# Gate logits of a mixture-of-experts layer from 12 float32 products per image in place of 36 bf16 products

## The chip, the cores and the metric

The kernel runs on one core of a Trainium2 chip. The metric is the device time of one execution in microseconds (us), lower is better.

## The reference

The input x is float32, 32 images of 384 channels and 28 x 28 = 784 pixels. The output is x plus a mixture of experts of its group normalisation:

```python
def _gn(v, G=32, eps=1e-5):
    B_, C_, H_, W_ = v.shape
    g = v.reshape(B_, G, C_ // G, H_, W_)
    m = jnp.mean(g, axis=(2, 3, 4), keepdims=True)
    s = jnp.var(g, axis=(2, 3, 4), keepdims=True)
    return ((g - m) / jnp.sqrt(s + eps)).reshape(v.shape)

x_flat = x.transpose(0, 2, 3, 1).reshape(-1, c)
scores = jax.nn.softmax(x_flat @ gate_w + gate_b, -1)      # 4 experts
top_v, top_i = jax.lax.top_k(scores, 2)
top_w = jax.nn.softmax(top_v, -1)
present = (top_i[:, :, None] == jnp.arange(e)[None, None, :]).any(0)
coef = jnp.einsum('ke,kbhw->ebhw', present.astype(x.dtype), wmap)
hdn = jax.nn.relu(jnp.einsum('bchw,edc->ebdhw', x, w1) + b1)
y = jnp.einsum('ebdhw,eod->ebohw', hdn, w2) + b2
out = jnp.einsum('ebohw,ebhw->bohw', y, coef)
```

`present` says of each rank (first or second choice) and expert whether any pixel at all chose it; the coefficient of an expert is the sum of the weights of the ranks in which it is present. The gate logits decide which expert is first and second, so they are computed with float32 accuracy.

## The kernel before

**Tiles.** Channels lie on the 128 partitions, three to a partition (NJ = 3). The images are taken in 8 groups of 4 (IMAGES). The 3136 pixels of a group are cut into 7 tiles of T = 448 pixels, and a tile times an expert is a unit: 28 units in a group, 224 in all. A unit has three chunks (NK) of the hidden dimension. For unit u TensorE computes `mm1(u + 1)`, that is 27 products of 448 columns into `z_ps`, and then `mm2(u)`, 27 products into `y_ps` (lines 444 to 486). Each float32 operand is held as two float32r numbers, `hi` and `lo` = value - `hi`, and each product is made of three: hi x lo, lo x hi, hi x hi. Between the two, VectorE scales a chunk by the coefficient row into `hid` (`scale`, line 508), ScalarE makes `h_hi` (line 515) and VectorE `h_lo` (line 519).

**Preparation of an image.** While one image is computed the next is prepared: VectorE takes statistics (`stats`, `group_stats`), GpSimd raises the variance to the power -0.5 (line 289), VectorE normalises the image in place in `x_raw`, half by half (line 303). ScalarE rounds it to `x_hi` (line 331), VectorE makes `x_lo` (line 335). For the gate the normalised half is split further into three bf16 parts, `x_part`: ScalarE casts part 1 (`part1`, line 308), VectorE subtracts it (`less_part1`, line 314), ScalarE casts part 2 (`part2`, line 319), VectorE subtracts that into part 3 (`part3`, line 323). The gate weights are split in the same way once (lines 605 to 608), and the three parts of the 4 experts stand in 12 of 32 stationary columns, `gw_part`.

**The gate product** (lines 338 to 348) is TensorE's: 3 parts x 3 channel slices x 4 quarters of the image. A quarter has 196 pixels, and its product is put at its own column tile of 32, so that its result stands in partitions 32 g to 32 g + 31 of one bank. ScalarE copies the result (`gate_copy`), VectorE transposes it, adds up the three parts (line 363) and the bias, and finds the two best (`gate_logits`, `gate_top2`, `gate_weights`, `gate_coefs`). The coefficient rows `wrow` go to HBM (`rows_out`) and come back broadcast over partitions (`rows_in`).

**What sets the order.** Every engine has its instructions in an order written out by hand, with semaphores between them. On VectorE and ScalarE the steps of the next image stand behind given chunks: `preparing` (line 567) turns the chunk number q into an offset `off` = q - (21 k - 30) for image k of the group, and `group` places, for example, `less_part1` of the first half at `off` 5, `part3` at 7 and 9, `gate_logits` at 12, and the second `split_x_lo` at `HI1[k]` + 1. TensorE has the gate product of image k ahead of `mm1` of unit 7 (k - 1) + 1, and that of image 1 ahead of unit 3. SyncE issues all loads and stores. `next_image` (line 909) waits until `x_lo` of the image that holds the place in `x_raw` is made. The numbers `SCAN_LINKS`, `IMAGE_LINKS` and `DVE_LINKS` count VectorE's chained steps for its own semaphore.

**The start.** Image 0 is prepared alone, while the weights arrive and are split (`weight_hi` on ScalarE, line 761, `weight_lo` on GpSimd, line 847). TensorE first runs WARM = 8 float32 products of 128 columns on a tile of ones (line 975). VectorE counts which experts were picked in image 0; if one is missing for a rank, a scan over the other images follows (not taken with this input). Image 1 is prepared in the first chunks of group 0 (`prepare_first`).

Of the kernel before, what the change touches and what calls it, by code (L numbers as in the profile page):

```python
# [21 lines left out]
PARTS = 3  # L22
# [8 lines left out]
WARM = 8  # L31
SCAN_LINKS = 38
IMAGE_LINKS = 32
# [21 lines left out]
def conv_moe(nc, x, gate_w, gate_b, w1, b1, w2, b2, out):  # L55
    f32, f32r, bf16, i32 = mybir.dt.float32, mybir.dt.float32r, mybir.dt.bfloat16, mybir.dt.int32
# [6 lines left out]
    with ctx:  # L63
# [14 lines left out]
        gw_part = sb("gw_part", [P, NJ, 32], bf16)  # L78
        gw_rest = sb("gw_rest", [P, 2, NJ, E])
# [7 lines left out]
        x_part = sb("x_part", [P, PARTS, HALVES, NJ, HALF], bf16)  # L87
        xn_rest = sb("xn_rest", [P, NJ, HALF])
# [8 lines left out]
        def slab_of(tile, i):  # L97
# [9 lines left out]
        early_rest = rows[:, 1, 1:1 + EARLY].rearrange("p r t -> p (r t)")[:, 0:NJ * HALF].rearrange(  # L107
            "p (j t) -> p j t", j=NJ)
# [83 lines left out]
        class Sems:  # L192

            def __init__(self, pre):
# [4 lines left out]
                self.part1_ready = sem(pre + "part1_ready")  # L199
                self.rest_ready = sem(pre + "rest_ready")  # L200
                self.part2_ready = sem(pre + "part2_ready")
                self.part3_ready = sem(pre + "part3_ready")
# [95 lines left out]
        def rest_of(h, alone):  # L298
            return early_rest if alone and h == 1 else xn_rest[:, :, :]

# [4 lines left out]

        def part1(act, s, n, q, h):
            act.wait_ge(s.xn_ready, HALVES * n + h + 1)
            nc.scalar.copy(x_part[:, 0, h], x_raw[:, q, :, half(h)]).then_inc(s.part1_ready, 1)  # L308

        def less_part1(dve, s, n, q, h, alone=False):  # L310
            dve.wait_ge(s.part1_ready, HALVES * n + h + 1)
            if h == 1 and not alone:
                dve.wait_ge(s.part3_ready, HALVES * n + 1)
            nc.vector.tensor_tensor(rest_of(h, alone), x_raw[:, q, :, half(h)], x_part[:, 0, h],  # L314
                                    ALU.subtract).then_inc(s.rest_ready, 1)

        def part2(act, s, n, h, alone=False):
            act.wait_ge(s.rest_ready, HALVES * n + h + 1)
            nc.scalar.copy(x_part[:, 1, h], rest_of(h, alone)).then_inc(s.part2_ready, 1)  # L319

        def part3(dve, s, n, h, alone=False):
            dve.wait_ge(s.part2_ready, HALVES * n + h + 1)
            nc.vector.tensor_tensor(x_part[:, 2, h], rest_of(h, alone), x_part[:, 1, h],  # L323
                                    ALU.subtract).then_inc(s.part3_ready, 1)
# [256 lines left out]
        def _(dve):  # L581
# [4 lines left out]
            nc.vector.memset(gw_part[:, :, :], 0.0)  # L586
# [12 lines left out]
            for i in range(NJ * HALVES):  # L599
# [30 lines left out]
            with dve.If(flag > 0):  # L630
                nc.vector.memset(pad[:, :], 0.0).then_inc(scan_free, 1)
                with dve.Fori(1, B) as b:
# [6 lines left out]
                    for h in range(HALVES):  # L639
                        normalise(dve, scan, n, 1, h)  # L640
                        less_part1(dve, scan, n, 1, h)
                        part3(dve, scan, n, h)
# [28 lines left out]
            def prepare_first(G, q, lk):  # L671
# [8 lines left out]
                if q == 2:  # L680
                    normalise(dve, main, 1, 1, 1)
                    less_part1(dve, main, 1, 1, 0)
                if q == 3:
                    split_x_lo(dve, 1, 1, 0)
                    part3(dve, main, 1, 0)
                    less_part1(dve, main, 1, 1, 1)
                if q == 4:
                    split_x_lo(dve, 1, 1, 1)
                    part3(dve, main, 1, 1)
# [9 lines left out]
            def group(G):  # L699
                lk = Links(dve, dve_step, G.g * DVE_LINKS + START[0] + (0 if G.first else EARLY_LINKS))  # L700
                for q in range(CHUNKS):
# [10 lines left out]
                    for k, off in preparing(G, q):  # L712
# [12 lines left out]
                        if off == 5:  # L725
                            less_part1(dve, main, n, slot, 0)
                        if off == 7:
                            part3(dve, main, n, 0)
                            less_part1(dve, main, n, slot, 1)
                        if off == 9:  # L730
                            part3(dve, main, n, 1)
# [25 lines left out]
        def _(act):  # L757
# [7 lines left out]
            for h in range(HALVES):  # L765
                part1(act, main, 0, 0, h)
            for h in range(HALVES):
                part2(act, main, 0, h, True)
            for h in range(HALVES):
# [15 lines left out]
            with act.If(flag > 0):  # L785
                with act.Fori(1, B) as b:
                    n = b - 1
                    for h in range(HALVES):
                        part1(act, scan, n, 1, h)
                        part2(act, scan, n, h)  # L790
# [3 lines left out]
            def prepare_first(G, q):  # L794
                if q == 2:
                    part1(act, main, 1, 1, 0)
                    split_x_hi(act, 1, 1, 0)
                if q == 3:
                    part2(act, main, 1, 0)
                    part1(act, main, 1, 1, 1)  # L800
                    split_x_hi(act, 1, 1, 1)
                if q == 4:
                    part2(act, main, 1, 1)
# [7 lines left out]
            def group(G):  # L811
                for q in range(CHUNKS):
# [3 lines left out]
                    for k, off in preparing(G, q):  # L816
                        n, slot = G.image(k), k % SLOTS
                        if off == 4:
                            part1(act, main, n, slot, 0)
                        if off == 5:  # L820
                            part1(act, main, n, slot, 1)
                        if off == 6:
                            part2(act, main, n, 0)
                        if off == 8:
                            part2(act, main, n, 1)
# [205 lines left out]
```

## Time and profile before

| | |
|---|---|
| median of 3 executions | 2565.67 us |
| lowest and highest | 2565.27 and 2566.45 us |
| profiled execution, its own time | 2567.38 us |
| its span, first to last instruction | 2565.6 us |
| mean granted clock of TensorE | 0.996 of full speed |
| TensorE busy | 2519.3 us, 98% of the span |
| VectorE busy | 1623.8 us, 63% |
| ScalarE busy | 630.7 us, 25% |
| DMA queue of loads and stores | 187.81 MB, 25.7% of 16 engines |

The span lies 1.8 us under that execution's own time. Busy shares are averages over stages with different limits: the first 110 us and the rest have to be read apart. Engines are named PE (TensorE), PEld (its weight loads), DVE (VectorE), ACT (ScalarE), POOL (GpSimd) and SP (SyncE); L344 is line 344 of the kernel before. An entry `A <- B` in a list of waits says that A's engine sat idle until B was done. Matmuls are pipelined: a duration of 0.36 us overlaps the next, and the distance between starts is what a product costs.

### The profile page before, as it was taken

To read this page: it belongs to the slowest core of one execution; us is meant where nothing else is said; L and a number is where in the kernel's file an instruction comes from. 1 tells how busy PE (TensorE), PEld (TensorE's weight loads), DVE (VectorE), ACT (ScalarE), POOL (GpSimd) and SP (SyncE) were. 2 spreads that over 40 slices of the span, in tenths; PEclk is the share of its full clock that TensorE was granted. 3 is DMA by queue.
4 is the path that set the end of the run, shared out by engine and by line. 5 is a ranking of instruction groups with operands and counts; after the bars stand their busy time and mean duration, and the time that the engine had idled before them with its cause. 6 is when DMAs were issued, how large, how long until landed. Compare 5 with 4: busy or idle time off the path is not lost.

```text
span 2565.6 us, 34840 instructions
## 1 busy us (share of the span) xinstructions
PE 2519.3 (98%) x13266; PEld 2302.0 (90%) x13266; DVE 1623.8 (63%) x3293; ACT 630.7 (25%) x973; POOL 74.4 (3%) x44
## 2 busy tenths in 40 slices
PE   4899999999999999999999999999999999999999
PEld 3799999999999999999999999999999999999998
DVE  7766666666666657665666666576666666665643
ACT  3322222222222222222222222222222222222211
POOL 3000000000000000000000000000000000000000
PEclk9999999999999999999999999999999999999999
DMA  4322123222133221232311322203322123231120
GB/s 161 89 78 71 52 70 89 78 82 59 52 89 93 67 79 55 69 100 68 92 55 46 100 78 82 80 25 97 89 71 78 51 72 100 61 91 51 46 75 22
DMA packets 193439, 190.15 MB, mean 74 GB/s; under 512 B 29808, under 2 KB 191856, under 8 KB 193264
## 3 DMA queue, kind: packets, MB, share of 16 engines
q1 hardware_dynamic: 193264, 187.81, 25.7%
q8 instruction: 111, 1.82, 0.3%
q14 instruction: 64, 0.52, 0.1%
HBM read 146.03 MB, written 41.75 MB: 73 GB/s over the span
## 4 chain that ended last, share of the span: by engine, by line
PE 96%; DVE 2%; DMA 1%; issue 1%; POOL 0%; ACT 0%; SPq 0%; DVEq 0%; POOLq 0%; ACTq 0%
PE y_ps L479 16%; PE y_ps L481 16%; PE z_ps L460 16%; PE y_ps L480 16%; PE z_ps L462 16%; PE z_ps L461 16%; PE g_ps L344 1%; DMA b_sb<-in_b 0%; DMA rows<-rows_dram 0%; DVE h_lo L519 0%; DVE x_part L323 0%; DVE x_lo L335 0%; POOL w_lo L847 0%; DVE x_raw L303 0%; DMA rows_dram<-wrow 0%
## 5 line engine op out<-in xcount | busy, mean ns | idle before, releaser
L508 DVE SCALAR_TENSOR_TENSOR hid<-z_ps,b_sb,rows 128x448 f32<-128x448 f32 x668 | 453.5, 679 | 753.9 <-PE z_ps L462 739.7
L479 PE MATMUL y_ps<-h_lo,w_hi 128*128 128x448 f32 x2016 | 741.8, 368 | 13.4 <-DVE h_lo L519 13.1
L460 PE MATMUL z_ps<-x_lo,w_hi 128*128 128x448 f32 x2016 | 743.4, 369 | 1.3 <-DVE x_lo L335 1.0
L481 PE MATMUL y_ps<-h_hi,w_hi 128*128 128x448 f32 x2016 | 741.1, 368 | 0.0
L480 PE MATMUL y_ps<-h_hi,w_lo 128*128 128x448 f32 x2016 | 740.9, 368 | 0.0
L462 PE MATMUL z_ps<-x_hi,w_hi 128*128 128x448 f32 x2016 | 736.7, 365 | 0.0
L461 PE MATMUL z_ps<-x_hi,w_lo 128*128 128x448 f32 x2016 | 736.5, 365 | 0.0
L515 ACT ACTIVATE h_hi<-hid 128x448 fp32r<-128x448 f32 x672 | 385.2, 578 | 1356.8 <-DVE hid L508 1343.2
L519 DVE SCALAR_TENSOR_TENSOR h_lo<-hid,h_hi 128x448 fp32r<-128x448 f32 x672 | 413.6, 616 | 26.5 <-ACT h_hi L515 26.1
L479 PEld LDWEIGHTS y_ps<-h_lo,w_hi 128*128 128x128 f32 x2016 | 379.3, 188 | 50.4 <-DVE h_lo L519 14.4
L460 PEld LDWEIGHTS z_ps<-x_lo,w_hi 128*128 128x128 f32 x2016 | 379.9, 188 | 38.0 <-issue 7.1
L481 PEld LDWEIGHTS y_ps<-h_hi,w_hi 128*128 128x128 f32 x2016 | 379.4, 188 | 35.5
L480 PEld LDWEIGHTS y_ps<-h_hi,w_lo 128*128 128x128 f32 x2016 | 379.3, 188 | 34.8
L462 PEld LDWEIGHTS z_ps<-x_hi,w_hi 128*128 128x128 f32 x2016 | 379.6, 188 | 33.1
L461 PEld LDWEIGHTS z_ps<-x_hi,w_lo 128*128 128x128 f32 x2016 | 380.2, 189 | 29.3
L534 DVE SCALAR_TENSOR_TENSOR res<-y_ps,bias,res 128x448 f32<-128x448 f32 x165 | 102.7, 677 | 101.7 <-PE y_ps L481 101.6
L289 POOL TENSOR_TENSOR rstd<-gvar_eps,minus_half 128x8 f32<-128x8 f32 x32 | 52.7, 1646 | 2286.3 <-DVE gvar_eps L284 2286.3
L319 ACT CAST x_part<-xn_rest 128x1176 bf16<-128x1176 f32 x63 | 73.9, 1173 | 135.7 <-DVE xn_rest L314 135.7
L526 DVE SCALAR_TENSOR_TENSOR res<-rows,bias_gap,res 128x448 f32<-128x448 f32 x168 | 104.7, 677 | 0.0
L308 ACT CAST x_part<-x_raw 128x1176 bf16<-128x1176 f32 x64 | 75.0, 1173 | 82.3 <-DVE x_raw L303 82.3
L267 DVE BATCH_NORM_STATS2 st<-x_raw 128x6 f32<-128x392 f32 x186 | 92.8, 554 | 2.3 <-DMA x_raw<-in_x 2.3
L314 DVE TENSOR_TENSOR xn_rest<-x_raw,x_part 128x1176 f32<-128x1176 f32 x63 | 86.9, 1380 | 3.5 <-ACT x_part L308 0.2
(97 smaller groups left out, 695.6 us busy)
## 6 DMA issues: line engine op xcount, KB each, us to landing
rows<-rows_dram SPq DMA_DIRECT2D x78, 560.0 KB, 7.4
x_raw<-in_x SPq DMA_DIRECT2D x62, 588.0 KB, 7.4
res<-in_x SPq DMA_DIRECT2D x80, 336.0 KB, 3.5
out<-res SPq DMA_DIRECT2D x78, 336.0 KB, 3.1
rows<-rows_dram SPq DMA_DIRECT2D x16, 840.0 KB, 7.2
res<-in_x SPq DMA_DIRECT2D x16, 504.0 KB, 5.8
out<-res SPq DMA_DIRECT2D x16, 504.0 KB, 6.0
rows<-rows_dram SPq DMA_DIRECT2D x16, 280.0 KB, 6.6
```

What stands on the lines that cost most here:

```text
L267: ins = nc.vector.bn_stats(st6[:, HALVES * j + h], x_raw[:, q, j, half(h)])
L460: nc.tensor.matmul(z, w1_hi[:, e, j, ks], lo, start=(j == 0), stop=False)
L461: nc.tensor.matmul(z, w1_lo[:, e, j, ks], hi, start=False, stop=False)
L462: ins = nc.tensor.matmul(z, w1_hi[:, e, j, ks], hi, start=False, stop=(j == NJ - 1))
L479: nc.tensor.matmul(y, w2_hi[:, e, k, ms], h_lo[:, slot], start=first, stop=False)
L480: nc.tensor.matmul(y, w2_lo[:, e, k, ms], h_hi[:, slot], start=False, stop=False)
L481: ins = nc.tensor.matmul(y, w2_hi[:, e, k, ms], h_hi[:, slot], start=False, stop=last)
L508: nc.vector.scalar_tensor_tensor(hid[:, q % HIDS], z_ps[:, q % ZB, 0:T], b1_sb[:, e, k:k + 1], coef, ALU.add, ALU.mult).then_inc(scaled, 1)
L515: nc.scalar.activation(h_hi[:, q % RING], hid[:, q % HIDS], ACT.Relu).then_inc(hhi_ready, 1)
L519: nc.vector.scalar_tensor_tensor(h_lo[:, q % RING], hid[:, q % HIDS], 0.0, h_hi[:, q % RING].bitcast(f32), ALU.max, ALU.subtract).then_inc ...
L526: lk.inc(nc.vector.scalar_tensor_tensor(xs, rows[:, G.slot(t), E], bias_gap[:, m:m + 1], xs, ALU.mult, ALU.add))
L534: nc.vector.scalar_tensor_tensor(xs, y_ps[:, m, 0:T], bias01[:, 1, m:m + 1], xs, ALU.add, ALU.add).then_inc(out_ready, 1)
```

## The change

The gate product multiplies the normalised pixels themselves, as they stand in `x_raw` in float32, with float32 gate weights padded to 32 columns (`gw_pad`): 3 channel slices x 4 quarters = 12 instructions, at the same column tiles. The three-part split of pixels and weights goes, with its four steps per half image (`part1`, `less_part1`, `part2`, `part3`), its buffers and semaphores, and the sum over the three parts in `gate_logits`. TensorE's gate product waits for `xn_ready` in place of `part3_ready`; since it now reads `x_raw`, SyncE waits for `gate_ready` too before it loads another image into the place. The warm-up has 12 products in place of 8 and waits for `rstd_ready` in place of `part1_ready`. The core of the diff (the calls of the four steps, which also go in the scan, in `prepare_first` and in `group` of both engines, are left out):

```diff
--- before.py
+++ after.py
@@
-WARM = 8
-SCAN_LINKS = 38
-IMAGE_LINKS = 32
+WARM = 12
+SCAN_LINKS = 37
+IMAGE_LINKS = 31
@@
-        gw_part = sb("gw_part", [P, NJ, 32], bf16)
-        gw_rest = sb("gw_rest", [P, 2, NJ, E])
+        gw_pad = sb("gw_pad", [P, NJ, 32])
@@
-        x_part = sb("x_part", [P, PARTS, HALVES, NJ, HALF], bf16)
-        xn_rest = sb("xn_rest", [P, NJ, HALF])
@@
-        def gate_product(pe, s, n):
-            pe.wait_ge(s.part3_ready, HALVES * (n + 1))
-            for t in reversed(range(PARTS)):
-                for j in range(NJ):
-                    for g in range(4):
-                        h, at = divmod(g * QUART, HALF)
-                        ins = nc.tensor.matmul(g_ps[32 * g:32 * (g + 1), 0:QUART], gw_part[:, j],
-                                               x_part[:, t, h, j, at:at + QUART],
-                                               start=(t == PARTS - 1 and j == 0), stop=(t == 0 and j == NJ - 1),
-                                               tile_position=(0, 32 * g))
+        def gate_product(pe, s, n, q):
+            pe.wait_ge(s.xn_ready, HALVES * (n + 1))
+            for j in range(NJ):
+                for g in range(4):
+                    ins = nc.tensor.matmul(g_ps[32 * g:32 * (g + 1), 0:QUART], gw_pad[:, j],
+                                           x_raw[:, q, j, g * QUART:(g + 1) * QUART],
+                                           start=(j == 0), stop=(j == NJ - 1), tile_position=(0, 32 * g))
             ins.then_inc(s.gate_ready, 1)
@@
-            lk.link(nc.vector.tensor_reduce(
-                lg[:, :, :], lg_pix[:, :, 0:PARTS * E].rearrange("p c (t e) -> p c e t", e=E), AX.X, ALU.add))
-            lk.link(nc.vector.tensor_tensor(lg[:, :, :], lg[:, :, :], over_pixels(gb[:, :]), ALU.add))
+            lk.link(nc.vector.tensor_tensor(lg[:, :, :], lg_pix[:, :, 0:E], over_pixels(gb[:, :]), ALU.add))
@@
-            lk.link(nc.vector.tensor_copy(gw_part[:, :, 0:E], gw_in[:, :, :]))
-            lk.link(nc.vector.tensor_tensor(gw_rest[:, 0], gw_in[:, :, :], gw_part[:, :, 0:E], ALU.subtract))
-            lk.link(nc.vector.tensor_copy(gw_part[:, :, E:2 * E], gw_rest[:, 0]))
-            nc.vector.tensor_tensor(gw_part[:, :, 2 * E:3 * E], gw_rest[:, 0], gw_part[:, :, E:2 * E],
-                                    ALU.subtract).then_inc(gw_ready, 1)
+            nc.vector.tensor_copy(gw_pad[:, :, 0:E], gw_in[:, :, :]).then_inc(gw_ready, 1)
@@
             for h in range(HALVES):
                 normalise(dve, main, 0, 0, h)
-            for h in range(HALVES):
-                less_part1(dve, main, 0, 0, h, True)
-            for h in range(HALVES):
-                part3(dve, main, 0, h, True)
@@
-            def next_image(b, place_free, k):
+            def next_image(b, place_free, gate_done, k):
                 sp.wait_ge(main.xlo_ready, place_free)
+                sp.wait_ge(main.gate_ready, gate_done)
@@
             pe.wait_ge(gw_ready, 1)
-            pe.wait_ge(main.part1_ready, 1)
+            pe.wait_ge(main.rstd_ready, 1)
             for _ in range(WARM):
                 nc.tensor.matmul(g_ps[:, 0:P], ones[:, :], ones[:, :], start=True, stop=True)
```

TensorE's instructions at the start, `ones` being the warm-up tile; the same replacement of the row of gate products stands at each of the 32 gate products. Before:

```order
L970 UNCONDITIONAL_BRANCH
L975 MATMUL g_ps<-ones 128x128 x8
L344 MATMUL g_ps<-x_part,gw_part 32x196 x36
L460 MATMUL z_ps<-x_lo,w_hi 128x448
L461 MATMUL z_ps<-x_hi,w_lo 128x448
L462 MATMUL z_ps<-x_hi,w_hi 128x448
```

and after the change:

```order
L895 UNCONDITIONAL_BRANCH
L900 MATMUL g_ps<-ones 128x128 x12
L309 MATMUL g_ps<-x_raw,gw_pad 32x196 x12
L422 MATMUL z_ps<-x_lo,w_hi 128x448
L423 MATMUL z_ps<-x_hi,w_lo 128x448
L424 MATMUL z_ps<-x_hi,w_hi 128x448
```

The row of 36 became one of 12 whose moving operand is `x_raw`; nothing moved against the z products.

VectorE's instructions during the preparation of image 1, from the second half's normalisation on. Before:

```order
L303 TENSOR_SCALAR x_raw<-x_raw,norm 128x3x392
L314 TENSOR_TENSOR xn_rest<-x_raw,x_part 128x1176
L508 SCALAR_TENSOR_TENSOR hid<-z_ps,b_sb,rows 128x448
L519 SCALAR_TENSOR_TENSOR h_lo<-hid,h_hi 128x448
L335 TENSOR_TENSOR x_lo<-x_raw,x_hi 128x3x392
L323 TENSOR_TENSOR x_part<-xn_rest,x_part 128x1176
L314 TENSOR_TENSOR xn_rest<-x_raw,x_part 128x1176
L508 SCALAR_TENSOR_TENSOR hid<-z_ps,b_sb,rows 128x448
L519 SCALAR_TENSOR_TENSOR h_lo<-hid,h_hi 128x448
L526 SCALAR_TENSOR_TENSOR res<-rows,bias_gap,res 128x448 x3
L335 TENSOR_TENSOR x_lo<-x_raw,x_hi 128x3x392
L323 TENSOR_TENSOR x_part<-xn_rest,x_part 128x1176
```

and after the change:

```order
L290 TENSOR_SCALAR x_raw<-x_raw,norm 128x3x392
L470 SCALAR_TENSOR_TENSOR hid<-z_ps,b_sb,rows 128x448
L481 SCALAR_TENSOR_TENSOR h_lo<-hid,h_hi 128x448
L302 TENSOR_TENSOR x_lo<-x_raw,x_hi 128x3x392
L470 SCALAR_TENSOR_TENSOR hid<-z_ps,b_sb,rows 128x448
L481 SCALAR_TENSOR_TENSOR h_lo<-hid,h_hi 128x448
L488 SCALAR_TENSOR_TENSOR res<-rows,bias_gap,res 128x448 x3
L302 TENSOR_TENSOR x_lo<-x_raw,x_hi 128x3x392
L470 SCALAR_TENSOR_TENSOR hid<-z_ps,b_sb,rows 128x448
```

The two L314 and the two L323 are gone; the rest keeps its order.

## Rows read from the trace of the kernel before

**Rows 1.** The page: busy us of each engine, and TensorE's granted clock in 40 slices

```profile
PE 2519.3 (98%) x13266; PEld 2302.0 (90%) x13266; DVE 1623.8 (63%) x3293; ACT 630.7 (25%) x973; POOL 74.4 (3%) x44
...
PEclk9999999999999999999999999999999999999999
```

**Rows 2.** Waits of TensorE, whole run: us in total, times, longest us

```profile
PE g_ps L975 <- ACT x_part L308: 22.2, 1, 22.2
PE y_ps L479 <- DVE h_lo L519: 13.1, 5, 6.4
```

**Rows 3.** The same, from 115 us to 2565 us

```profile
PE y_ps L479 <- DVE res L534: 0.3, 1, 0.3
PE g_ps L344 <- issue: 0.3, 1, 0.3
```

**Rows 4.** Timeline of TensorE, last gate product: start us, us, what, count

```profile
2411.70 0.36 PE L481 MATMUL y_ps<-h_hi,w_hi 128*128 128x448 f32 x1
2411.99 0.94 PE L344 MATMUL g_ps<-x_part,gw_part 128*32 128x196 bf16 x36
2412.86 0.48 PE L460 MATMUL z_ps<-x_lo,w_hi 128*128 128x448 f32 x1
2413.18 0.37 PE L461 MATMUL z_ps<-x_hi,w_lo 128*128 128x448 f32 x1
```

**Rows 5.** Instructions of the tile g_ps: count, duration ns min/median/max

```profile
L344 PE MATMUL g_ps<-x_part,gw_part x1152: 247/248/373, 27.5 to 2412.7; 128*32 128x196 bf16 x192
L352 ACT COPY lg_rows<-g_ps x32: 322/322/323, 29.2 to 2413.0; 128x196 f32<-128x196 f32 x32
...
L975 PE MATMUL g_ps<-ones x16: 421/421/552, 22.2 to 25.6; 128*128 128x128 f32 x16
```

**Rows 6.** Timeline of TensorE in the start, clock at 1.2 GHz: warm-up and first gate product

```profile
22.79 2.13 PE L975 MATMUL g_ps<-ones 128*128 128x128 f32 x9
...
27.47 1.66 PE L344 MATMUL g_ps<-x_part,gw_part 128*32 128x196 bf16 x36 [1.49 <-DVE x_part L323]
```

**Rows 7.** Groups by line, 115 to 2565 us, VectorE and ScalarE: busy us, mean ns

```profile
L314 DVE TENSOR_TENSOR xn_rest<-x_raw,x_part 128x1176 f32<-128x1176 f32 x60 | 82.8, 1380 | 3.1
...
L323 DVE TENSOR_TENSOR x_part<-xn_rest,x_part 128x1176 bf16<-128x1176 f32 x60 | 82.6, 1376 | 0.0
...
L308 ACT CAST x_part<-x_raw 128x1176 bf16<-128x1176 f32 x60 | 70.4, 1173 | 74.6 <-DVE x_raw L303 74.6
...
L331 ACT CAST x_hi<-x_raw 128x1176 fp32r<-128x1176 f32 x60 | 69.6, 1160 | 0.0
```

**Rows 8.** Timeline of VectorE, image 0

```profile
17.84 4.04 DVE L303 TENSOR_SCALAR x_raw<-x_raw,norm 128x1176 f32<-128x1176 f32 x2
...
27.34 2.67 DVE L335 TENSOR_TENSOR x_lo<-x_raw,x_hi 128x1176 fp32r<-128x1176 f32 x2
29.92 0.41 DVE L362 STREAM_TRANSPOSE lg_pix<-lg_rows 128x224 f32<-128x224 f32 x1
30.36 0.25 DVE L363 TENSOR_REDUCE lg<-lg_pix 128x28 f32<-128x84 f32 x1
```

**Rows 9.** Timeline of GpSimd, third split of weights

```profile
17.44 2.61 POOL L847 TENSOR_TENSOR w_lo<-res,w_hi 128x1152 fp32r<-128x1152 f32 x1
```

**Rows 10.** Timeline of TensorE, preparation of image 1

```profile
82.08 0.47 PE L479 MATMUL y_ps<-h_lo,w_hi 128*128 128x448 f32 x1 [3.41 <-DVE h_lo L519]
...
84.97 1.62 PE L344 MATMUL g_ps<-x_part,gw_part 128*32 128x196 bf16 x36
```

**Rows 11.** Timeline of TensorE, second and last product of two units of mm2

```profile
115.97 0.37 PE L480 MATMUL y_ps<-h_hi,w_lo 128*128 128x448 f32 x1
...
121.04 0.36 PE L481 MATMUL y_ps<-h_hi,w_hi 128*128 128x448 f32 x1
...
126.95 0.37 PE L480 MATMUL y_ps<-h_hi,w_lo 128*128 128x448 f32 x1
...
132.11 0.37 PE L481 MATMUL y_ps<-h_hi,w_hi 128*128 128x448 f32 x1
```

More of the change, by code:

```diff
@@ L21 @@
 GJ = -(-QUART // 32)
-PARTS = 3
 ROWS = E + 1
@@ L55, in conv_moe @@
 def conv_moe(nc, x, gate_w, gate_b, w1, b1, w2, b2, out):
-    f32, f32r, bf16, i32 = mybir.dt.float32, mybir.dt.float32r, mybir.dt.bfloat16, mybir.dt.int32
+    f32, f32r, i32 = mybir.dt.float32, mybir.dt.float32r, mybir.dt.int32
     ALU, ACT, AX = mybir.AluOpType, mybir.ActivationFunctionType, mybir.AxisListType
@@ L106, in conv_moe @@
         early = rows[:, 1, 1:1 + EARLY]
-        early_rest = rows[:, 1, 1:1 + EARLY].rearrange("p r t -> p (r t)")[:, 0:NJ * HALF].rearrange(
-            "p (j t) -> p j t", j=NJ)
         st6 = sb("st6", [P, NJ * HALVES, 6])
@@ L198, in __init__ @@
                 self.xn_ready = sem(pre + "xn_ready")
[L199 to L202, printed above, removed]
                 self.xhi_ready = sem(pre + "xhi_ready")
@@ L296, in norm_columns @@
                                         back[:, :, :, :].rearrange("p a g f -> p (a g f)")))
-        def rest_of(h, alone):
-            return early_rest if alone and h == 1 else xn_rest[:, :, :]
         def normalise(dve, s, n, q, h):
@@ L304, in normalise @@
                                     ALU.subtract, ALU.mult).then_inc(s.xn_ready, 1)
[L306 to L324, printed above, removed]
         def ring(q, h):
@@ L585, in _ @@
             nc.vector.memset(ones[:, :], 1.0)
-            nc.vector.memset(gw_part[:, :, :], 0.0)
+            nc.vector.memset(gw_pad[:, :, :], 0.0)
             nc.vector.memset(lg_rows[:, :], 0.0)
@@ L640, in _ @@
                         normalise(dve, scan, n, 1, h)
-                        less_part1(dve, scan, n, 1, h)
-                        part3(dve, scan, n, h)
                     gate_logits(dve, scan, n, sk)
@@ L681, in prepare_first @@
                     normalise(dve, main, 1, 1, 1)
-                    less_part1(dve, main, 1, 1, 0)
                 if q == 3:
                     split_x_lo(dve, 1, 1, 0)
-                    part3(dve, main, 1, 0)
-                    less_part1(dve, main, 1, 1, 1)
                 if q == 4:
                     split_x_lo(dve, 1, 1, 1)
-                    part3(dve, main, 1, 1)
                 if q == 6:
@@ L724, in group @@
                             normalise(dve, main, n, slot, 1)
[L725 to L731, printed above, removed]
                         if off == 11:
@@ L765, in _ @@
             for h in range(HALVES):
[L766 to L769, printed above, removed]
                 split_x_hi(act, 0, 0, h)
@@ L787, in _ @@
                     n = b - 1
-                    for h in range(HALVES):
-                        part1(act, scan, n, 1, h)
-                        part2(act, scan, n, h)
                     gate_copy(act, scan, n)
@@ L795, in prepare_first @@
                 if q == 2:
-                    part1(act, main, 1, 1, 0)
                     split_x_hi(act, 1, 1, 0)
                 if q == 3:
-                    part2(act, main, 1, 0)
-                    part1(act, main, 1, 1, 1)
                     split_x_hi(act, 1, 1, 1)
-                if q == 4:
-                    part2(act, main, 1, 1)
                 if q == 5:
@@ L817, in group @@
                         n, slot = G.image(k), k % SLOTS
[L818 to L825, printed above, removed]
                         if off == 10:
@@ L899, in _ @@
             sp.wait_ge(main.xlo_ready, HALVES)
+            sp.wait_ge(main.gate_ready, 1)
             for h in range(HALVES):
@@ L924, in group @@
                         place_free = held(G.image(k + 1) * HALVES)
+                        gate_done = held(G.image(k + 1))
                         b = held(G.image(k + 2))
@@ L929, in group @@
                         if t == 0:
-                            next_image(b, place_free, 3)
+                            next_image(b, place_free, gate_done, 3)
                         rows_out(sp, coefs, k)
@@ L938, in group @@
                         if not G.last and t:
-                            next_image(b, place_free, k + 2)
+                            next_image(b, place_free, gate_done, k + 2)
                     elif t < TILES - 1:
@@ L945, in group @@
                         place_free = held(G.image(5) * HALVES)
+                        gate_done = held(G.image(5))
                         b = held(G.image(6))
@@ L949, in group @@
                         rows_in(sp, G, t + 1)
-                        next_image(b, place_free, 6)
+                        next_image(b, place_free, gate_done, 6)
                     if t:
@@ L972, in _ @@
             pe.wait_ge(gw_ready, 1)
-            pe.wait_ge(main.part1_ready, 1)
+            pe.wait_ge(main.rstd_ready, 1)
             for _ in range(WARM):
                 nc.tensor.matmul(g_ps[:, 0:P], ones[:, :], ones[:, :], start=True, stop=True)
-            gate_product(pe, main, 0)
+            gate_product(pe, main, 0, 0)
             start = Group(0, 0, 0, first=True)
@@ L985, in _ @@
                 with pe.Fori(1, B) as b:
-                    gate_product(pe, scan, b - 1)
+                    gate_product(pe, scan, b - 1, 1)
                 sum_counts(pe, scan)
@@ L993, in group @@
                     if u % (UNITS // IMAGES) == 0 and not (G.last and k == IMAGES) and not (G.first and k == 1):
-                        gate_product(pe, main, G.image(k))
+                        gate_product(pe, main, G.image(k), k % SLOTS)
                     if G.first and u == 2:
-                        gate_product(pe, main, 1)
+                        gate_product(pe, main, 1, 1)
                     if u < UNITS - 1:
```

## The prediction

> **What bounds the kernel.** I began with the page. TensorE is busy for 98% of the span and its granted clock stands at full speed in every slice [rows 1]. Busy says little by itself, since the ends of matmuls are modelled, so I asked next what TensorE waits for. Over the whole run it is 22.2 us before the first product and 13.1 us in five waits for `h_lo` [rows 2]; from 115 us on, over 2450 us, two waits of 0.3 us are left [rows 3]. So there are two regimes. In the steady part the time is the sum of what TensorE streams, and work taken off VectorE or ScalarE gives nothing back there. In the first 110 us TensorE waits for a serial preparation of images 0 and 1, and there removed work can count in full. The timelines of both parts give the terms.
>
> **What one gate product costs now.** At 2411.99 us the 36 bf16 products take 0.94 us, the last of them 0.248 us long. From the last `y` product before to the second `z` product after are 1.48 us, where two ordinary steps of 0.203 us would be 0.41: it adds 1.07 us to TensorE's stream [rows 4, 5]. First start to last start is 0.94 - 0.248 = 0.69 us. Streamed one by one at 2.4 GHz, 36 times 196 columns would take 2.94 us. So the four column tiles run side by side: nine rounds of four, 0.69 / 8 = 0.086 us a round, of which 196 columns are 0.082. At 1.2 GHz the same is (1.66 - 0.37) / 8 = 0.161 us a round [rows 6].
>
> **What a float32 product costs.** The trace of before has float32 products only as warm-up: 8 instructions leave 16 records, so each is two [rows 5]. Nine of them take 2.13 us, the last 0.42, hence (2.13 - 0.42) / 8 = 0.214 us a record for 128 columns at 1.2 GHz [rows 6]: two cycles per column, two records, four times the streaming of bf16. A record of 196 columns at 2.4 GHz is then 2 x 196 / 2.4 = 0.163 us, with the 0.003 that the bf16 rounds carry 0.166 us. An image now needs 24 such records. No row shows float32 records in column tiles, so their overlap is the unknown, and it has three values:
> - Four at a time: 6 rounds, 6 x 0.166 = 1.00 us against 9 x 0.086 = 0.77; +0.23 us an image.
> - One at a time: 24 x 0.166 = 3.98 us; +3.21 us an image.
> - Two at a time: the two records of an instruction stand next to each other and use the same tile. If products start in program order, the second record of tile 0 waits until the first has streamed, and tile 1's first record waits behind it; only then do these two run together, and so on. 12 instructions make 13 rounds, 13 x 0.166 = 2.16 us; +1.39 us an image.
>
> I take the third. The bf16 rounds prove that tiles overlap, and nothing in them shows a product overtaking an earlier one: their order 0, 1, 2, 3, 0 never asks for it. The Trainium skill states the rule in TensorE: Matmul & The Clock Gate, section The mechanism: matmuls start and end strictly in program order. By it the sum has the +1.39; the rows of before agree but can't refute it. From the other side the same section prices a pack of tiles as one matmul's duration plus 4 ns for each further tile; by it the sum would have +0.23.
>
> **The sum, steady part.** All 32 images have a gate product, of which 31 (image 1 and later) stand in TensorE's stream: 31 x 1.39 = +43.1 us. Per image the change also takes two subtractions of 1.38 us and two more of the same length off VectorE, and four casts of some 1.17 us off ScalarE [rows 7]. That is 0: TensorE doesn't wait there [rows 3], and where those engines wait, it is for TensorE. ScalarE's `gate_copy` will wait 1.39 us longer with the `h_hi` behind it; TensorE has the 27 products of the next mm1, 5.5 us, before it needs that `h_lo`, so 0 again. SyncE's new wait on `gate_ready` stands behind the wait for `x_lo` of the same image. By the program's table the second half of `x_lo` is made some chunks after the gate product was issued, so what is queued behind (`rows_out`, `rows_in`, the store) is not held; 0.
>
> **The sum, start, image 0.** Now the second normalisation ends at 17.84 + 4.04 = 21.88 us; then come part 1, two subtractions, part 2, two more, `x_lo` (done at 30.0) and the logits at 29.92 [rows 8]. After the change the second `x_hi` (1.16 us [rows 7]) and the second `x_lo` (1.38, a subtraction of the same size) follow directly: 24.4 us, 5.5 earlier. The gate product starts at 21.9 and by 13 rounds takes 2.2 us, or 4.2 at 1.2 GHz; with the copy's 0.32 [rows 5] the logits begin between 24.5 and 26.5. I take the middle: -4.5 us. The normalisation itself may come earlier: it stood behind GpSimd's third `w_lo` (17.44 + 2.61 = 20.05 [rows 9]), and three small conversions ahead of it fall away. That is 0 to -2.6 us, one such `w_lo`; I take 0, since its second half may still meet the third. Four more warm-up products run where TensorE waits anyway; 0.
>
> **Image 1.** In the wait of 3.41 us at 82.08, and the stretch before it, VectorE is the chain [rows 10]. It loses four operations that start 1.30 us apart (the pair of `x_lo` in 2.67 us shows the spacing [rows 8]): -5.2 us. The shorter logits save the reduction of 0.25 us for each of both images: -0.5. Its gate product ran at 1.2 GHz (1.62 us [rows 10]); whether the next does I can't say, 0 with 2 us either way. The start gives -4.5 - 5.2 - 0.5 = -10.2 us, within -8 to -15.
>
> **A term of unknown sign.** `y` products stand 5.07 / 25 = 0.203 us apart in one unit and 5.16 / 25 = 0.206 in another, with the same shapes [rows 11]. I found no engine or transfer that goes with it. Over 6048 `y` products the difference is 22 us in all; a new gate product may shift which units get which. I take 0 and 5 us either way.
>
> **Sum:** +43.1 - 10.2 = +32.9 us on the profiled execution's own 2567.38 gives 2600.3. That execution was 1.7 us over the median of 2565.67, so the forecast is **2599 us**, its own range 2587 to 2611.
>
> **Rivals.**
> 1. Four at a time (ends faster). For it: the bf16 rounds, four of which start within some nanoseconds. Against it: the pairs of records on one tile. The price is 31 x 0.23 = +7.1, and the start gives its full -5.5 - 5.2 - 0.5 = -11.2, as the gate product hides under `x_lo`: -4.1 us, 2562 us. The point of decision is a gate product of 0.77 + 11.2 / 31 = 1.13 us; below it the change wins, above it loses.
> 2. One at a time: the tile position doesn't do for float32 what it does for bf16, so "12 in place of 36" is 24 serial records. For it: no float32 record in the trace overlaps another. Against it: those all used the full array. The price is 31 x 3.21 = +99.5; image 0's logits gain only about 2, so the start gives -7.7: +91.8 us, 2657 us.
> 3. The relief of VectorE and ScalarE speeds the steady part up. It would need waits of TensorE, and these are 0.3 us [rows 3]; I give it nothing of its own.
>
> **Chances.** Two at a time 0.50, four at a time 0.32, one at a time 0.18. A measurement tells 0.2%, some 5 us, from no change. Two and one at a time are slower by more. Four at a time, -4.1 us with about 5 either way, I split into 0.14 faster, 0.17 the same, 0.01 slower. So faster 0.14, same 0.17, slower 0.69. The range reaches down to hold the four-at-a-time case with its spread and leaves the serial one out: 2554 to 2613 us.
>
> **What would show it.** Starts within one gate product of the changed kernel: pairs 0.166 us apart, 13 rounds, some 2.3 us from the gate's start to the first `z` product, is my case; four starts within some nanoseconds and 1.1 us is the first rival; 24 single starts and 4.1 us the second. Right for the start: `x_lo` of image 0 done near 24.4 us, the wait at 82 us about 10 us earlier, and TensorE's waits from there to the end still under 1 us. I would be wrong in another way if TensorE began to wait for `h_lo` after a gate product, or if loads of `x_raw` came late behind `gate_ready`.

## The result, and the profile after the change

| | before | after |
|---|---|---|
| median | 2566.44 us (20 executions) | 2562.07 us (20) |
| lowest and highest | 2564.87 and 2567.21 | 2560.94 and 2563.33 |
| profiled execution, its span | 2565.6 us | 2560.6 us |

The ratio is 0.9983, 95% interval 0.9977 to 0.999: 4.4 us faster, near the edge of what can be told from no change. I had forecast 2599 us. The time came out where the first rival had it (2562 us), so the question is whether its mechanism did, too.

The page of the changed kernel, busy time of each engine, against [rows 1]:

```profile
PE 2524.1 (99%) x12890; PEld 2297.9 (90%) x12890; DVE 1453.8 (57%) x3130; ACT 487.3 (19%) x845; POOL 74.3 (3%) x44
```

VectorE lost 170 us of work and ScalarE 143, and the span lost 5. TensorE's waits over the whole run (us in total, times, longest), against [rows 2]:

```profile
PE g_ps L900 <- POOL rstd L279: 12.7, 1, 12.7
...
PE y_ps L441 <- DVE h_lo L481: 10.4, 5, 6.6
```

The list also has TensorE waiting 5.3 us for image 0's count of picked experts (`cnt`), 4.5 before. From 115 us to the end it has `g_ps` on "issue" with 0.3 us, as in [rows 3]: the steady part is TensorE's stream still.

TensorE's timeline at the last gate product (start us, us, what, records), against [rows 4], and at the gate products of images 2, 1 and 0, the chain of image 1 and the warm-up, against [rows 6, 10]:

```profile
12.65 5.05 PE L900 MATMUL g_ps<-ones 128*128 128x128 f32 x24 [12.65 <-POOL rstd L279]
...
21.47 2.19 PE L309 MATMUL g_ps<-x_raw,gw_pad 128*32 128x196 f32 x24 [3.77 <-DVE x_raw L290]
...
70.96 0.47 PE L441 MATMUL y_ps<-h_lo,w_hi 128*128 128x448 f32 x1 [1.16 <-DVE h_lo L481]
...
73.00 1.20 PE L309 MATMUL g_ps<-x_raw,gw_pad 128*32 128x196 f32 x24
...
131.04 1.20 PE L309 MATMUL g_ps<-x_raw,gw_pad 128*32 128x196 f32 x24
...
2407.02 0.36 PE L443 MATMUL y_ps<-h_hi,w_hi 128*128 128x448 f32 x1
2407.31 1.20 PE L309 MATMUL g_ps<-x_raw,gw_pad 128*32 128x196 f32 x24
2408.45 0.47 PE L422 MATMUL z_ps<-x_lo,w_hi 128*128 128x448 f32 x1
```

A gate product takes 1.13 us from its start to the first `z` product, where 36 bf16 products took 0.87 [rows 4]: +0.26, not +1.39. The row merges its 24 records (a record is one pass of a product in the trace; a float32 product leaves two). Their starts one by one, ns from the first, show the rounds, that is, the four records that run side by side:

```
   0    6   13   20
 190  196  203  210
 355  362  369  375
 521  528  535  541
 687  694  700  707
 853  860  866  873
```

Six rounds of four, the tiles of a round 6.6 ns apart, the rounds 0.166 us apart after a first step of 0.190. The trace doesn't name a record's tile; I give the records to the tiles in turn, which `tile_first` below tests. Then the second record of tile 0 stands at 190 ns, and tile 1's first record, later in the program, starts at 6 ns and so overtakes it.

VectorE's timeline, image 0 (columns as above), against [rows 8]:

```profile
15.46 5.96 DVE L290 TENSOR_SCALAR x_raw<-x_raw,norm 128x1176 f32<-128x1176 f32 x2
21.34 2.72 DVE L302 TENSOR_TENSOR x_lo<-x_raw,x_hi 128x1176 fp32r<-128x1176 f32 x2
24.08 0.41 DVE L326 STREAM_TRANSPOSE lg_pix<-lg_rows 128x224 f32<-128x224 f32 x1
```

**Where the time went.** The gate product of image 2 marks the start of the steady part. Before, TensorE's timeline there has:

```profile
143.36 0.94 PE L344 MATMUL g_ps<-x_part,gw_part 128*32 128x196 bf16 x36
```

| stretch | before, us | after, us | difference |
|---|---|---|---|
| up to the gate product of image 2 | 143.36 | 131.04 | -12.3 |
| from there to that of image 31 | 2268.63 | 2276.27 | +7.6 |
| the rest of the span | 153.6 | 153.3 | -0.3 |

The middle row is 29 images at 78.23 us before and 78.49 after: +0.26 each, the gate product's own extra. The mean step between products (starts less than 260 ns apart) hides two changes that cancel: a `z` product goes from 203.04 to 204.56 ns, a `y` product from 205.23 to 203.52. Over 6048 of each that is +9 and -10 us.

### The profile page after: what moved, and what is told of

Read it like the earlier page. It is cut to its first block, busy times and chain, and to the rows that moved or that the text cites. A ratio compares the mean times of both kernels' runs of the same rounds, so it can differ in the third digit from the quotient of the medians.

```text
span 2560.6 us, 33748 instructions
## 1 busy us (share of the span) xinstructions
PE 2524.1 (99%) x12890; PEld 2297.9 (90%) x12890; DVE 1453.8 (57%) x3130; ACT 487.3 (19%) x845; POOL 74.3 (3%) x44
## 4 chain that ended last, share of the span: by engine, by line
PE 96%; DVE 2%; DMA 1%; issue 1%; POOL 0%; ACT 0%; SPq 0%; DVEq 0%; POOLq 0%; ACTq 0%
PE z_ps L422 16%; PE z_ps L423 16%; PE z_ps L424 16%; PE y_ps L442 16%; PE y_ps L443 16%; PE y_ps L441 16%; PE g_ps L309 1%; DMA rows<-rows_dram 0%; DVE x_raw L290 0%; DMA x_raw<-in_x 0%; DVE h_lo L481 0%; DVE x_lo L302 0%; POOL w_lo L768 0%; POOL rstd L279 0%; DMA rows_dram<-wrow 0%
## 5 line engine op out<-in xcount | busy, mean ns | idle before, releaser
L302 DVE TENSOR_TENSOR x_lo<-x_raw,x_hi 128x1176 fp32r<-128x1176 f32 x64 | 88.2, 1378 | 0.0
L298 ACT CAST x_hi<-x_raw 128x1176 fp32r<-128x1176 f32 x64 | 74.3, 1162 | 9.5 <-DVE x_raw L290 9.5
L290 DVE TENSOR_SCALAR x_raw<-x_raw,norm 128x1176 f32<-128x1176 f32 x64 | 73.7, 1153 | 1.2
```

## Experiments

Each comparison of times has its own executions of the kernel before, at 2566.4 to 2566.6 us.

### Does a column tile wait for another? (tile_first)

The 12 products are the same, taken tile by tile.

```diff
-            for j in range(NJ):
-                for g in range(4):
+            for g in range(4):
+                for j in range(NJ):
```

> The changed kernel with the loops of the gate product exchanged: column tile outside, channel slice inside, so that the six records of a tile stand together. Theory A (a product waits only for the one before it on its own tile and may start ahead of products of other tiles, which is how the 24 float32 records came to run in six rounds of four): a gate product still takes 1.13 us to the first z product and the time stays at 2562 us within 3. Theory B (products start strictly in program order; the changed kernel got its rounds of four because its low and high records reach the engine tile by tile): records on one tile can't overlap, 24 x 0.166 = 3.98 us a gate product, 31 x 2.9 = +89 us, about 2650 us.

Measured: 2595.04 us, ratio 1.011 (1.0095 to 1.0126). TensorE's timeline, last gate product:

```profile
2438.68 2.27 PE L309 MATMUL g_ps<-x_raw,gw_pad 128*32 128x196 f32 x24
2440.87 0.47 PE L422 MATMUL z_ps<-x_lo,w_hi 128*128 128x448 f32 x1
```

2.20 us from start to `z`, between the two expectations. The starts, in ns:

```
0 190 356 361 521 551 687 717 723 853 883 913
1049 1079 1085 1215 1245 1275 1411 1441 1576 1606 1772 1938
```

Tile 0 has the starts 0, 190, 356, 521, 687, 853, the steps of the changed kernel. The next tile begins at 361, the others at 723 and 1085: each 0.36 us after the one before it, right behind that tile's third start, when three of its records still wait. So a product overtakes earlier ones that wait for their own tile, but only a few may wait. Strict order, my premise, would give 21 rounds or 3.5 us (the expectation's 3.98 let nothing at all overlap); it is refuted, whichever tile a record is given to. Tiles with unlimited queues would give 1.13 us; they are refuted, too. The count of three goes by tile: when tile 2 begins at 723 ns, tile 1 has three records waiting and tile 0 still its last. In the changed kernel a tile has one record waiting when the next tile's first starts, so the limit isn't met. What in the engine sets it was not tested.

### The same with bf16 (bf16_tile_first)

The kernel before, its 36 products taken tile by tile: nine to a tile.

```diff
-            for t in reversed(range(PARTS)):
-                for j in range(NJ):
-                    for g in range(4):
+            for g in range(4):
+                for t in reversed(range(PARTS)):
+                    for j in range(NJ):
```

> The kernel before with its gate product's loops exchanged: column tile outside, the nine bf16 products of a tile together. What the float32 run with tiles outside showed: each tile's first record started 0.36 us after the tile's before, at the moment its third of six records started, so a later tile starts once three records of the tile before are left waiting. Theory A (a few records wait per tile, others overtake them): with nine products, a tile starts when the sixth of the tile before starts, 5 x 0.085 = 0.43 us later; the gate product lasts 3 x 0.43 + 9 x 0.085 = 2.05 us in place of 0.77, +1.28 us, 31 of them +40 us, about 2606 us. Theory B (strict program order for bf16, overtaking for the two records of a float32 instruction alone): tiles don't overlap, 36 x 0.085 = 3.06 us, 31 x 2.3 = +71 us, 2637 us.

Measured: 2607.05 us, ratio 1.0157 (1.014 to 1.0174). TensorE's timeline, last gate product:

```profile
2451.74 2.24 PE L344 MATMUL g_ps<-x_part,gw_part 128*32 128x196 bf16 x36
2453.91 0.47 PE L460 MATMUL z_ps<-x_lo,w_hi 128*128 128x448 f32 x1
```

2.17 us in place of 0.87. The second tile's first start comes at 0.438 us, 6 ns behind the first tile's sixth (0.432): again three of its nine are left waiting. The rule read from the float32 records foretold what this adds to a gate product within 0.02 us (+1.28, measured +1.30) and is no matter of float32.

### What is a gate product worth? (gate_twice)

Every gate product is done twice in a row. The second pass starts its sum anew and overwrites the first with the same values.

```diff
-            for j in range(NJ):
+            for j in (0, 1, 2, 0, 1, 2):
```

> The changed kernel with each gate product computed twice in a row (the second overwrites the first with the same values). If each microsecond of it counts in full on TensorE's stream: six further rounds of 0.166 us, 31 x 1.00 = +31 us, 2593 us. If a part of it lies in idle time of TensorE (behind a wait that would be there anyway), less, down to 0.

Measured: 2598.38 us, ratio 1.0127 (1.0112 to 1.0143). TensorE's timeline, last gate product, and two pieces of the chain that ended last (start us, us, what):

```profile
2441.26 2.20 PE L309 MATMUL g_ps<-x_raw,gw_pad 128*32 128x196 f32 x48
2443.38 0.47 PE L422 MATMUL z_ps<-x_lo,w_hi 128*128 128x448 f32 x1
```

```profile
1006.63 2.37 issue
...
1644.91 2.37 issue
```

Start to `z` is 2.13 us: +1.00 for six more rounds of 0.166. 31 of them are 30.9 us, streamed in full. The other 5 us of the 36, which neither expectation had, are two pauses of 2.4 us with no releaser, 638 us apart, the length of two groups. Both stand inside the gate product of the second image of a group, just behind a turn of the loop over two groups. What stops TensorE there was not tested.

### Is the work taken off VectorE and ScalarE worth anything? (split_steady, split_start, place_h)

The changed kernel with the bf16 split of the pixels put back, its result read by nobody; the gate stays float32. `split_steady` does so for images 2 to 31, `split_start` for 0 and 1. Buffers, and where VectorE's steps stand in `split_steady` (the steps' code, as in the kernel before, ScalarE's casts and the places in `split_start` are left out):

```diff
+        x_part = sb("x_part", [P, 3, HALVES, NJ, HALF], bf16)
+        xn_rest = sb("xn_rest", [P, NJ, HALF])
         rows = sb("rows", [P, 2, ROWS, T])
...
+                        if off == 5:
+                            less_part1(dve, main, n, slot, 0)
+                        if off == 7:
+                            part3(dve, main, n, 0)
+                            less_part1(dve, main, n, slot, 1)
+                        if off == 9:
+                            part3(dve, main, n, 1)
```

> The changed kernel with the three-part bf16 split made again for images 2 to 31, into a buffer that nobody reads: four more operations on VectorE and four on ScalarE for each. Theory: in the steady part it lies beside TensorE's stream and is worth nothing, 0 within 1 us apart from what moved addresses do. Rival: relief of VectorE and ScalarE is what paid for part of the dearer gate product; then +2 to +8 us.

> The changed kernel with the three-part bf16 split made again for images 0 and 1 alone, into a buffer that nobody reads; the gate product stays float32. Theory: the start's gain of 12.3 us in the trace is the split work that is gone. Then +10 to +13 us, 2573 us. Rival: the gain comes from the earlier warm-up and clock; then under +4 us.

Measured: 2572.37 us (1.0022, 1.0013 to 1.0031) and 2586.51 us (1.0076, 1.0061 to 1.0092). In `split_steady` the image-2 gate product and TensorE's waits from 115 us on:

```profile
130.67 1.20 PE L337 MATMUL g_ps<-x_raw,gw_pad 128*32 128x196 f32 x24
```

```profile
PE z_ps L452 <- issue: 0.3, 1, 0.3
```

TensorE waits no more than before, and yet the kernel is 10 us slower. The `y` products are it: 205.37 ns in place of 203.52. The new buffers move `rows`, `res`, `hid`, `h_hi` and `h_lo`. `place_h` moves them as far without any work:

```diff
+        gap1 = sb("gap1", [P, 18816 // 4])
         rows = sb("rows", [P, 2, ROWS, T])
```

> The changed kernel with 18816 unused bytes per partition ahead of rows, res, hid, h_hi and h_lo, so that these stand some 18.8 KB further on, as in the run with the split made for images 2 to 31; no work is added. Theory (the step of the y products, 203.5 ns in the changed kernel and 205.4 ns in that run, goes by the place of the h buffers in SBUF): y step 205.4 ns, +10 us, 2572 us. Rival (the added work on VectorE and ScalarE slowed TensorE): y step 203.5, 2562 us.

Measured: 2571.9 us (1.0021, 1.0012 to 1.0031), `y` at 205.37, `z` at 204.43: the same 10 us. So the steady part's work is worth nothing (0.5 us between the two runs), and the place of the buffers 10 us. In `split_start` the step is the same, and the start is longer:

```profile
145.22 1.20 PE L337 MATMUL g_ps<-x_raw,gw_pad 128*32 128x196 f32 x24
```

```profile
PE z_ps L450 <- DVE x_lo L330: 8.5, 1, 8.5
```

The gate product of image 2 starts 14.2 us later than in the changed kernel. Less the placement's 10, which the expectation left out, some 14 us of the 24 are the split in the start. So work in the start counts, as forecast, and the rival of warm-up and clock (under 4 us) falls. It is a little more than the 10 to 13 expected, and than the 12.3 by which the kernel before was behind; here TensorE waited 8.5 us for `x_lo`, where the kernel before waited 1.0, so my order of the steps, halves one after the other, may be the dearer one.

### Is it the place of the buffers? (place_before, place_mixed, place_mixed32, place_mixed64)

The changed kernel with all moving operands, and `rows`, `res` and `hid` with them, where the kernel before has them:

```diff
-        gw_pad = sb("gw_pad", [P, NJ, 32])
+        gap0 = sb("gap0", [P, 72])
...
+        gw_pad = sb("gw_pad", [P, NJ, 32])
+        gap1 = sb("gap1", [P, 18432 // 4])
         rows = sb("rows", [P, 2, ROWS, T])
```

> The changed kernel with every buffer of x, rows, res, hid and h at the very address it has in the kernel before (the gate weights moved into the gap). Theory of place: the steps are those of before, z 203.0 ns and y 205.2 (1.5 ns less and 1.7 more than in the changed kernel), 6048 of each, -9 and +10 us: 2563 us. Rival: the steps follow from what the engines do beside TensorE; then z stays at 204.6.

`place_mixed` has `x_raw`, `x_hi` and `x_lo` at the addresses of before and `rows`, `res`, `hid`, `h_hi` and `h_lo` at those of after; the other two move the latter by 32 and 64 bytes more (`gap1` of 128 and 160 bytes).

```diff
-        gw_pad = sb("gw_pad", [P, NJ, 32])
+        gap0 = sb("gap0", [P, 72])
...
+        gap1 = sb("gap1", [P, 96 // 4])
         rows = sb("rows", [P, 2, ROWS, T])
...
         h_lo = sb("h_lo", [P, RING, T], f32r)
+        gw_pad = sb("gw_pad", [P, NJ, 32])
```

> The changed kernel with x_raw, x_hi and x_lo at their addresses of before and rows, res, hid and h at those of the changed kernel. Theory of place, each product's step set by its own moving buffer: z 203.0 and y 203.5 ns, -9 us, 2553 us. Rival: the step of one kind depends on what the other kind left (a phase that is handed on); then one of the two goes up again and the sum stays near 2562.

> The run with x at its addresses of before and h at those of the changed kernel (2558 us, z 203.0, y 204.4 ns), with rows, res, hid and h 32 bytes further on, so that h stands at a multiple of 64 bytes as x does. If the step goes by the place within 64 or 128 bytes, y falls to the 202.6 ns of the fast units of before or rises to 206.7 in all; if it goes by larger distances, nothing changes.

> The same with 64 bytes in place of 32: h at 32 bytes past a multiple of 64, as in the run at 2558 us. If the place within 64 bytes decides: y 204.4 ns and 2558 us again. If the place within 128 bytes or larger decides: another step of y.

| kernel | us | ratio, 95% | `z`, ns | `y`, ns |
|---|---|---|---|---|
| before | 2566.4 | | 203.04 | 205.23 |
| after | 2562.1 | 0.9983 | 204.56 | 203.52 |
| `place_h` | 2571.9 | 1.0021 | 204.43 | 205.37 |
| `place_before` | 2563.5 | 0.9989, 0.9979 to 0.9998 | 203.03 | 205.26 |
| `place_mixed` | 2558.0 | 0.9966, 0.9954 to 0.9979 | 202.98 | 204.42 |
| `place_mixed32` | 2563.0 | 0.9986, 0.9977 to 0.9996 | 203.04 | 205.24 |
| `place_mixed64` | 2560.9 | 0.9979, 0.9969 to 0.9988 | 203.15 | 204.79 |

`place_before` gives back both steps of the kernel before, to 0.03 ns, and the pattern from unit to unit in `y` (206.7 or 202.6, the same in 209 of 222 units). The steps account for the times: `place_mixed` against after is 6048 x (0.90 - 1.58) ns = -4.1 us, measured -4.1. A second and last product of one `z` unit, 25 steps apart, in the kernel before, the changed one and `place_mixed`:

```profile
1172.32 0.37 PE L461 MATMUL z_ps<-x_hi,w_lo 128*128 128x448 f32 x1
...
1177.40 0.36 PE L462 MATMUL z_ps<-x_hi,w_hi 128*128 128x448 f32 x1
```

```profile
1163.90 0.37 PE L423 MATMUL z_ps<-x_hi,w_lo 128*128 128x448 f32 x1
...
1169.01 0.37 PE L424 MATMUL z_ps<-x_hi,w_hi 128*128 128x448 f32 x1
```

```profile
1162.35 0.36 PE L425 MATMUL z_ps<-x_hi,w_lo 128*128 128x448 f32 x1
...
1167.41 0.36 PE L426 MATMUL z_ps<-x_hi,w_hi 128*128 128x448 f32 x1
```

5.08, 5.11 and 5.06 us. The `z` step follows the place of `x`: 203.0 to 203.2 in the five kernels that have it as before, 204.4 to 204.6 in the two others. The rule for `y` stays open: it has 203.52 in the changed kernel and 204.42 in `place_mixed`, with `h_hi` at the same address, so `x` or the `z` products have a part in it. That is half of what the rival in the expectation said, and the time of 2558.0 lies between its 2562 and my 2553. `place_mixed64` refutes a rule by the place within 64 bytes (`y` 204.79, not 204.42). But `place_mixed32` and `place_before` have `h` 18,688 bytes apart, 73 times 256, and the same `y` step in 209 of 222 units: a pattern that repeats every 128 or 256 bytes would fit, which no run tested. Nor did one move `h` without `rows`, `res` and `hid`. `place_mixed` is the best version found, 8.4 us under the kernel before.

### What holds the first normalisation? (pool_late)

In the changed kernel two normalisations take 5.96 us, while GpSimd makes `w_lo`. Here GpSimd waits for them.

```diff
             inverse_std(pool, main, 0)
+            pool.wait_ge(main.xn_ready, HALVES)
```

> The changed kernel with GpSimd's first w_lo held back until both halves of image 0 are normalised. In the changed kernel the two normalisations (1.1 us each elsewhere) take 5.96 us from 15.46 us on, while GpSimd makes w_lo. If they wait for GpSimd, they end some 5 to 6 us earlier, and the start gains what the later w_lo doesn't give back: -1 to -5 us. If they were slow for another reason: 0, or +2 to +6 us because w_lo comes later.

Measured: 2562.58 us (0.9985, 0.9976 to 0.9994), no different from the changed kernel. VectorE's timeline and GpSimd's:

```profile
12.55 2.09 DVE L290 TENSOR_SCALAR x_raw<-x_raw,norm 128x1176 f32<-128x1176 f32 x2
14.88 7.43 DVE L302 TENSOR_TENSOR x_lo<-x_raw,x_hi 128x1176 fp32r<-128x1176 f32 x2 [0.24 <-ACT x_hi L298]
```

```profile
14.72 6.35 POOL L769 TENSOR_TENSOR w_lo<-rows,w_hi 128x1152 fp32r<-128x1152 f32 x2 [2.70 <-DVE x_raw L290]
```

The normalisations gain 3.9 us and the two `x_lo` behind them lose 4.7. One by one, the overlapping spans of `pool_late` end in turns: `w_lo` at 17.37 us, `x_lo` at 18.61, `w_lo` at 21.07, `x_lo` at 22.31. An `x_lo` ends 1.24 us behind the other engine's operation and takes 1.38 when nothing runs beside it; a `w_lo` ends 2.46 behind and takes 2.61. So in these spans each of the two engines waits for the other's whole operation. A small operation is held as well: in the changed kernel, VectorE and GpSimd have

```profile
24.52 2.08 DVE L327 TENSOR_TENSOR lg<-lg_pix,gb 128x28 f32<-128x28 f32 x1
```

```profile
23.78 2.78 POOL L768 TENSOR_TENSOR w_lo<-res,w_hi 128x1152 fp32r<-128x1152 f32 x1 [3.19 <-ACT w_hi L702]
```

This `lg` takes 0.19 us in most images; here it ends at 26.60 us, 0.04 behind `w_lo`. Not every operation is held: in `pool_late` the reduction `lg_max` takes its 0.18 us at 24.90, inside a `w_lo`. The meeting was only moved: the first `z` product comes 1.8 us earlier than in the changed kernel (22.46 for 24.21), then TensorE waits 7.3 us for the count of image 0 in place of 5.3, and the first `y` product is 0.4 later.

### Does the longer warm-up matter? (warm8)

```diff
-WARM = 12
+WARM = 8
```

> The changed kernel with 8 warm-up products as before, in place of 12. Theory: the warm-up runs while TensorE waits for the normalisation; 0 within 1 us. Rival: the four more hold the clock up and are part of the start's gain; then +1 to +3 us, and the granted clock of the gate product or of the first z products differs.

Measured: 2561.2 us (0.9981, 0.9971 to 0.999), the same as with 12. TensorE's timeline:

```profile
11.84 3.75 PE L900 MATMUL g_ps<-ones 128*128 128x128 f32 x16 [11.84 <-POOL rstd L279]
...
20.65 2.19 PE L309 MATMUL g_ps<-x_raw,gw_pad 128*32 128x196 f32 x24 [5.05 <-DVE x_raw L290]
```

With 12 the granted clock rose to 2.4 GHz at 17.1 us and fell back at 20.5, with TensorE idle since 17.7 and the gate product still to come at 21.5; with 8 it first rose at 27.0. Both gate products of image 0 ran at 1.2 GHz, in 2.19 us. The four more products are worth nothing here, as forecast; a start without any warm-up was not run.

## Why the prediction was wrong

**The step that failed** is the choice under "What a float32 product costs": that "the second record of tile 0 waits until the first has streamed, and tile 1's first record waits behind it". It doesn't wait: tile 1 starts 6 ns after tile 0. So 13 rounds became 6, the forecast 2.3 us from the gate's start to the first `z` product became 1.13, and 31 x 1.39 = 43.1 us became 31 x 0.26 = 8.1. I had written that nothing in the bf16 rounds shows a product overtaking, and then took that silence for evidence. The Trainium skill, TensorE: Matmul & The Clock Gate, section The mechanism, says that matmuls start strictly in order; the starts of `tile_first` refute it for matmuls in different column tiles. Its price of a pack, one duration and 4 ns for each further tile, comes near what was measured: 6.6 ns a tile for float32 and 3 to 4 ns for bf16.

**The price of a record** was right: 0.166 us at 2.4 GHz. At 1.2 GHz the rounds stand 0.327 us apart. The rival's +0.23 became +0.26; the first step of 0.190 and the wider spacing of the tiles (6.6 ns in place of 3 to 4) make most of the difference. The 0.003 us that the prediction adds to a round isn't what its own sums give (0.086 - 0.082 = 0.004), but it is what was measured (0.166 - 0.163).

**The steady relief** was right at nothing: the waits did not change, and `split_steady` less its placement costs nothing. TensorE's list shows no wait behind `gate_copy` or `next_image`.

**The start** was -12.3 us against -10.2 forecast and -11.2 in the rival's case. Image 0's `x_lo` was done at 24.06 (forecast 24.4), the logits began at 24.08 (5.8 earlier), and the first `y` product came 6.0 earlier. The normalisation began 2.4 us earlier and ended only 0.5 earlier, since both its halves now met a `w_lo`. The other 6.3 are image 1: 5.5 forecast, and 0.4 of its gate product, which now meets 2.4 GHz (1.20 us, where [rows 10] has 1.62). The wait of 82.08 stands at 70.96 now, 1.16 us in place of 3.41. The prediction read full clock "in every slice" off the page; a slice is 64 us long, and the trace of before has the clock at 1.2 GHz until 35.2 us and in three later stretches up to 86.4 us, as the prediction's own 1.62 us for that product says.

**Luck in the rival's number.** That its 2562 us was met so closely is luck in part: its gate product was 1.0 us short over the run, its start 1.1 us short, and the placement, which it had at nothing, gave -1; the kernel before was 0.8 us slower over 20 executions than over the 3 that it started from.

**The term of unknown sign** was no noise. It follows the place of the buffers; ±5 us was fair for the sum (-1 here, as `z` and `y` cancel), but a single one of them moves 10 us.

**The point of decision** stood: 1.13 us was set on rounds alone (0.77 for bf16), and counted so the float32 product takes 6 x 0.166 = 1.00. From start to `z`, which is what the stream pays, the limit is 0.87 + 12.3 / 31 = 1.27 us. The measured 1.13 is 0.14 under it, and 31 times that is 4.3 us: the result.

## What to carry to other kernels

Where products go to different column tiles, order them so that a tile's turn comes again only after the others': then float32's two records cost little more than their streaming (1.13 us here), and the same products taken tile by tile cost twice as much (2.20 us). When a change costs little in a stream of thousands of products, compare the mean step of the untouched ones before any story is told: a buffer that moved can be worth more than the edit. On a kernel that waits only in its start, price removed work there and nowhere else.

## What was not expected of the hardware

- Products start out of program order across column tiles, with about three records left waiting for their tile before a later tile's may pass (the next tile begins 0.36 us later for six float32 records a tile, 0.44 for nine bf16 ones).
- The step of 448-column float32r products depends on where buffers lie: unit means of 202.4 to 206.7 ns, with the same shapes and no wait.
- VectorE and GpSimd hold each other up, and in `pool_late` they take turns. A normalisation goes from 1.09 to 3.06 us, an `x_lo` from 1.38 to 3.78, a `w_lo` from 2.61 [rows 9] to 3.78, and a copy of 128 x 32 (`back`) from 0.17 to 2.60.
- With 24 more gate records an image, two pauses of 2.4 us came up for which the profile shows no releaser.
